# The tail of a two-layer attention kernel: normalising by tile, sharing the products, and experts from two rounded parts

## The chip, the cores and the metric

The kernel runs on one core of a Trainium2 chip. The metric is the device time of one execution in microseconds. Before the change three runs took 314.24 us (median), 313.40 and 314.36 us. Five engines work side by side, each with its own list of instructions that it takes in order: TensorE (PE, matmuls), VectorE (DVE), ScalarE (ACT), GpSimd (POOL) and SyncE (SP, which issues most DMAs). They wait for one another with semaphores. Nothing is ordered by a compiler; the order of every engine is written in the source.

## The reference, cut to what matters

Four batches of 256 tokens, 128 wide, pass two layers.

```python
x = x + cross_attention(layernorm(x), ctx)     # 16 heads of 64, 512 context rows, RoPE on the keys,
                                               # scores clipped to +-11, softmax, out @ Wo + bo
h = layernorm(x)                               # the second layer works on h, and its result is added to x
h1 = rmsnorm(h) * gamma1
q = h1 @ Wq + bq                               # 16 heads of 8
k, v = split((h1 @ Wdown + bdown) @ Wup + bup)
att = softmax(einsum('bthd,btgd->bthg', q, k) / sqrt(8))   # heads g against heads h, per token
r = h + (einsum('bthg,btgd->bthd', att, v) @ Wo2 + bo2)
h2 = rmsnorm(r) * gamma2
gate = softmax(h2 @ Wg + bg)                   # 8 experts
y = r + einsum('btd,edf,bte->btf', h2, We, gate)
out = x + y
```

## The kernel before, in words

The first layer runs in 32 slots, one for each pair of heads of each batch (8 slots a batch, some 8 us each). In a slot TensorE computes key, query and value projections for later slots, the scores of this pair in two halves, and the product of the previous pair's weights with the values (`times_values`). ScalarE takes exponentials, GpSimd clips them and adds the rotated keys, VectorE multiplies keys by cosine and sine and forms the low parts of operands. Where a product shall be nearly exact and faster than a plain fp32 matmul, the operand is kept as two rounded parts (dtype fp32r): `split3` then issues three matmuls, high by high, high by low, low by high.

The second layer of a batch is worked in small steps between the slots of the next batch. A table (`POST_STEPS`) puts TensorE's steps at places in the slots; `OWN_STEPS` does it for the other engines. The steps of batch 3, and the last of batches 1 and 2, have no slots left: they are the tail, from about 266 us on. `TAIL_STEPS` is TensorE's order there, and gives each step one of eight PSUM banks (0 is `side`, 1 and 2 are the two halves of `sc`, 3 `own_bank`, 4 and 5 `pj_k`, 6 `pv`, 7 `sums`). The other engines' tails are written out in `last_batches` (VectorE, GpSimd) and in ScalarE's block. A step `x/0` or `x/1` is that of one tile of 128 tokens. The steps in their order:

- `norm0` to `norm3`: reciprocals of the softmax sums (`recS`) are spread over the 128 partitions of a pair by a matmul with `spread`; VectorE multiplies `u` by them into `on`. Each step covers two pairs, all 256 tokens.
- `out_proj/t`: eight fp32 matmuls with `wo`, after which VectorE takes statistics, GpSimd the root, VectorE writes `hn`.
- `h_T`, `down`, `query`, `keyval2`: transposes and small products. VectorE (tile 1) and GpSimd (tile 0) multiply queries and keys into `prod`; `logits` sums tile 0's on TensorE by adding with the identity as an operand; `outputs` does it for the weighted values.
- `o_T`, `out_proj2`, `h2_T`, `gate`: output projection, root norm, transposed `h2T`, gate logits.
- `moe0` to `moe3`: tile 0's experts 0 to 3 and 4 to 7, then tile 1's. Each is one fp32 matmul of 128x512 with `fwe`. For batches 0 to 2 ScalarE multiplies each expert by its gate into `moe` and GpSimd adds them up (`add_experts`). For batch 3 VectorE adds them one by one straight from PSUM (`mix_tile`), in two sums, which `add_residuals` joins.

`made(name)` means that TensorE has finished a step, `taken(name)` that its bank has been read.

Of the kernel before, what the change touches and what calls it, by code (L numbers as in the profile page):

```python
# [28 lines left out]
fp32r = mybir.dt.float32r  # L29
ALU = mybir.AluOpType  # L30
# [20 lines left out]
G = 16  # L51
# [26 lines left out]
    ("norm0", LAST, 1), ("norm1", LAST, 2), ("norm2", LAST, 4), ("norm3", LAST, 5),  # L78
    ("out_proj/0", LAST, 6), ("out_proj/1", LAST, 7),
    ("h_T/0", LAST, 0), ("down/0", LAST, 1), ("query/0", LAST, 2), ("keyval2/0", LAST, 4),  # L80
    ("h_T/1", LAST, 5), ("down/1", LAST, 0), ("o_T", LAST - 1, 1), ("keyval2/1", LAST, 6), ("query/1", LAST, 7),
    ("out_proj2", LAST - 1, 2), ("logits", LAST, 4), ("h2_T", LAST - 1, 0), ("gate", LAST - 1, 5),
    ("moe0", LAST - 1, 1), ("moe1", LAST - 1, 6), ("moe2", LAST - 1, 0), ("outputs", LAST, 2),
    ("o_T/0", LAST, 4), ("out_proj2/0", LAST, 7), ("moe3", LAST - 1, 5), ("o_T/1", LAST, 1), ("out_proj2/1", LAST, 6),
    ("h2_T/0", LAST, 2), ("gate/0", LAST, 4), ("moe0", LAST, 0), ("h2_T/1", LAST, 1), ("moe1", LAST, 2),
    ("gate/1", LAST, 4), ("moe2", LAST, 7), ("moe3", LAST, 5),
# [24 lines left out]
    "root_norm": [(11, "end")],  # L111
    "gate_exps": [(13, None)],
# [11 lines left out]
}  # L124

# [112 lines left out]
def xattn_ffn(nc, x, ctx, cos, sin, ln_lat_g, ln_lat_b, ln_ctx_g, ln_ctx_b, Wq, Wkv, Wo, bo,  # L238
              gamma1, f_Wq, f_bq, f_Wdown, f_bdown, f_Wup, f_bup, f_Wo, f_bo, gamma2, f_Wg, f_bg, f_We, out):
    es = ExitStack()  # L240
    with es:
# [50 lines left out]
        fwe = sb("fwe", [128, NE, D])  # L292
# [48 lines left out]
        q2 = sb("q2", [128, D])  # L341
        dT = sb("dT", [L, NT])
# [5 lines left out]
        h2T = sb("h2T", [128, NT])  # L348
# [29 lines left out]
        ld = {n: sem(f"ld_{n}") for n in ("wk", "trig", "x", "wv", "wq", "bias", "wo", "ffn")}  # L378
# [57 lines left out]
        s_hn2 = sem("s_hn2")  # L436
        s_x23 = sem("s_x23")
# [8 lines left out]
        s_weigh_1a = sem("s_weigh_1a")  # L446
        s_gden = sem("s_gden")
# [28 lines left out]
        def taken(name, b):  # L476

            k, n = SIDE[name, b]
            return s_side_free[k], n + 1

# [23 lines left out]
        def _(sp):  # L504
# [44 lines left out]
            for j in range(NPAIR):  # L549
# [3 lines left out]
                for dst, src, name in later[3 * j - 3:3 * j] if j else ():  # L553
                    sp.dma_start(dst, src).then_inc(ld[name], 16)
# [11 lines left out]
        def _(pe):  # L566
# [69 lines left out]
            def times_values(j):  # L636
# [3 lines left out]
                if j:  # L640
                    pe.wait_ge(s_u, j)
# [1319 lines left out]
```

## Time and profile before

| what | value |
|---|---|
| median of three runs | 314.24 us |
| the profiled execution, whole | 312.95 us |
| its span (first to last instruction) | 311.2 us |
| granted TensorE clock over the span | 0.998 of 2.4 GHz |
| sums of batch 3's last pairs start (tail) | 266.27 us |

The profile is of one execution. A span of 311.2 us stands against a time of 312.95 us: 1.75 us lie outside. The busy shares are averages over the whole kernel. In the tail it is the order of each engine's list and the waits that count, so the timeline and the chain of waits are read there. A fp32 matmul is shown as two instructions.

### The profile page before, as it was taken

The page shows a single profiled execution, that of the slowest core. Times are in us where ns is not written, and L with a number is a line of the kernel's source. Part 1 is how long each engine was busy: PE and PEld are TensorE (multiplying, and loading weights), DVE is VectorE, ACT ScalarE, POOL GpSimd, SP SyncE. Part 2 cuts the span into 40 slices and gives each one's busy share as a digit, 9 for nine tenths or more (in the row PEclk, how much of TensorE's full clock was granted, in tenths as well). Part 3 has the DMA queues.
Part 4 walks back from the last instruction along what each step waited for, and adds up shares of the span by engine and source line. Part 5 has one row for each costly group of instructions (what it writes and reads, how often), then busy time and mean ns, then how long its engine had stood idle before and what let it go on. Part 6 is the DMA issues. An engine that isn't in the chain of part 4 may idle for free.

```text
span 311.2 us, 6616 instructions
## 1 busy us (share of the span) xinstructions
PE 292.3 (94%) x2482; PEld 204.0 (66%) x2482; DVE 243.4 (78%) x449; ACT 162.7 (52%) x326; POOL 209.0 (67%) x208
## 2 busy tenths in 40 slices
PE   7898999999999999999999999999999999899983
PEld 6776576666668666666687676556686665476651
DVE  3985998875875849899787798977847699687856
ACT  3446466667443734774426465774436368314741
POOL 6446775665573838686737578498827597968764
PEclk9999999999999999999999999999999999999999
DMA  7554412211210201111201111111101200000001
GB/s 218 179 151 114 123 38 57 62 36 44 60 28 9 52 17 36 35 36 36 51 19 34 37 34 36 33 38 34 36 0 37 53 1 2 0 19 0 1 2 34
DMA packets 16319, 14.24 MB, mean 46 GB/s; under 512 B 4832, under 2 KB 11808, under 8 KB 16288
## 3 DMA queue, kind: packets, MB, share of 16 engines
q1 hardware_dynamic: 14992, 13.49, 16.6%
q10 hardware_dynamic: 1296, 0.33, 0.5%
q8 instruction: 20, 0.33, 0.5%
q14 instruction: 11, 0.09, 0.1%
HBM read 4.89 MB, written 0.52 MB: 17 GB/s over the span
## 4 chain that ended last, share of the span: by engine, by line
PE 52%; DVE 21%; POOL 9%; issue 8%; ACT 5%; SPq 3%; DMA 2%; POOLq 0%; ACTq 0%; DVEq 0%
PE pv L645 10%; PE sc L631 9%; PE sums L666 6%; PE pj_k L569 4%; PE side L751 4%; DVE ks L1286 3%; PE pj_k L571 3%; PE pj_k L570 3%; SPq L536 3%; POOL moe L1868 3%; POOL e L1806 3%; PE side L827 2%; DVE ksin L1350 2%; DMA kswap<-ksin 2%; DVE kcos L1350 2%
## 5 line engine op out<-in xcount | busy, mean ns | idle before, releaser
L1806 POOL TENSOR_SCALAR e<-e 128x1024 f32<-128x1024 f32 x64 | 71.6, 1119 | 60.7 <-ACT e L944 47.6
L944 ACT ACTIVATE e<-sc 128x1024 f32<-128x1024 f32 x64 | 65.6, 1024 | 28.1 <-PE sc L631 28.0
L631 PEld LDWEIGHTS sc<-qs,ks 64*128 64x128 f32 x768 | 49.6, 185 | 21.7 <-issue 18.5
L645 PE MATMUL pv<-e,v 128*64 128x256 f32 x512 | 62.3, 385 | 1.6 <-POOL e L1806 0.8
L631 PE MATMUL sc<-qs,ks 64*128 64x256 f32 x768 | 62.5, 295 | 0.4 <-ACT e L944 0.2
L1799 POOL TENSOR_TENSOR krot<-kcos,kswap 128x512 f32<-128x512 f32 x32 | 45.2, 1411 | 9.8 <-DMA kswap<-ksin 7.0
L645 PEld LDWEIGHTS pv<-e,v 128*64 128x64 f32 x512 | 34.1, 136 | 24.2 <-issue 7.2
L952 ACT ACTIVATE u<-pv 128x256 f32<-128x256 f32 x32 | 12.3, 386 | 62.2 <-PE pv L645 55.5
L1286 DVE TENSOR_TENSOR ks<-krot,ks 128x512 fp32r<-128x512 f32 x32 | 33.6, 1051 | 0.1
L1350 DVE TENSOR_TENSOR ksin<-pj_k,sinT 128x512 f32<-128x512 f32 x32 | 21.9, 685 | 3.4 <-PE pj_k L571 3.2
L936 ACT ACTIVATE v<-pj_k 128x512 f32<-128x512 f32 x28 | 16.8, 598 | 14.3 <-PE pj_k L571 13.9
L666 PE MATMUL sums<-e,sum_rows 128*32 128x256 f32 x384 | 23.2, 382 | 0.6 <-POOL e L1806 0.6
L1350 DVE TENSOR_TENSOR kcos<-pj_k,cosT 128x512 f32<-128x512 f32 x32 | 21.8, 680 | 0.0
L921 ACT ACTIVATE ks<-krot 128x512 fp32r<-128x512 f32 x32 | 20.1, 629 | 1.2 <-POOL krot L1799 1.1
L1286 DVE TENSOR_TENSOR qs<-pj_k,qs 128x256 fp32r<-128x256 f32 x32 | 13.4, 418 | 9.1 <-ACT qs L927 9.1
L1360 DVE TENSOR_TENSOR moe<-e 128x512 f32<-128x512 f32 x16 | 12.5, 794 | 8.8 <-POOL e L1806 8.8
L666 PEld LDWEIGHTS sums<-e,sum_rows 128*32 128x32 f32 x384 | 11.2, 109 | 9.2 <-issue 1.1
L1595 DVE TENSOR_REDUCE own_bank<-prod 128x64 f32<-128x1024 f32 x14 | 16.6, 1216 | 0.1
L1868 POOL TENSOR_TENSOR moe<-moe 128x512 f32<-128x512 f32 (+2 forms) x18 | 15.4, 855 | 1.0
L569 PE MATMUL pj_k<-ctxT,wkA 128*128 128x512 f32 x32 | 14.3, 446 | 1.0 <-DVE kcos L1350 0.5
L1242 POOL TENSOR_TENSOR prod<-att,kv 128x1024 f32<-128x1024 f32 x6 | 14.6, 2435 | 0.6 <-ACT att L1053 0.3
L1234 POOL TENSOR_TENSOR prod<-q,kv 128x1024 f32<-128x1024 f32 x6 | 14.3, 2382 | 0.5
(289 smaller groups left out, 560.4 us busy)
## 6 DMA issues: line engine op xcount, KB each, us to landing
kswap<-ksin SPq DMA_DIRECT2D x126, 64.0 KB, 2.0
ctx_in<-in_ctx_dram SPq DMA_DIRECT2D x4, 256.0 KB, 3.4
prod<-in_L_xattn_Wkv_dram SPq DMA_DIRECT2D x2, 512.0 KB, 6.0
x_in<-in_x_dram SPq DMA_DIRECT2D x1, 512.0 KB, 6.0
prod<-in_L_xattn_Wq_dram SPq DMA_DIRECT2D x1, 512.0 KB, 6.8
wo<-in_L_xattn_Wo_dram SPq DMA_DIRECT2D x1, 512.0 KB, 4.4
fwe<-in_L_ffn_We_dram SPq DMA_DIRECT2D x1, 512.0 KB, 4.4
out_dram<-x_in SPq DMA_DIRECT2D x3, 128.0 KB, 1.8
```

Source lines behind the costliest of these rows:

```text
L569: nc.tensor.matmul(out_ap, w_hi, m_hi, start=True, stop=False)
L631: last = nc.tensor.matmul(sc[:, h, c * NT:(c + 1) * NT], ks[rows, j % 3, k_part, chunk], qs[rows, j % 2, q_part, :], start=(k_part + q_par ...
L645: last = nc.tensor.matmul(pv_bank[DH * h:DH * h + DH, 0:NT], v[:, c, col:col + DH], e[:, j % 3, h, c, :], start=(c == 0), stop=(c == SC - 1))
L666: last = nc.tensor.matmul(sum_bank[32 * g:32 * g + 32, 0:NT], w, e_added[:, pair % 2, c, g % 2, :] if j < PAIRS else e[:, pair % 3, g % 2, ...
L921: nc.scalar.activation(ks[:, j % 3, 0, :], krot[:, j % 2, :], ACT.Copy).then_inc(s_khi, 1)
L936: nc.scalar.activation(v[:, c, 512 * half:512 * half + 512], value_bank(n)[:, :], ACT.Copy).then_inc(s_v, 1)
L944: nc.scalar.activation(e[:, j % 3, :, 2 * half:2 * half + 2, :].rearrange("p h c n -> p h (c n)"), sc[:, :, :], ACT.Exp, scale=SCALE).then ...
L1286: return nc.vector.tensor_tensor(dst, whole, f(hi), ALU.subtract)
L1350: nc.vector.tensor_tensor(dst[:, j % 2, :], key_bank(j)[:, :], trig[:, :], ALU.mult).then_inc(s_kmul, 1)
L1799: nc.gpsimd.tensor_tensor(krot[:, j % 2, :], kcos[:, j % 2, :], kswap[:, j % 2, :], ALU.add)\
L1806: nc.gpsimd.tensor_scalar(a, a, EXP_HIGH, EXP_LOW, ALU.min, ALU.max).then_inc(s_clip, 1)
L1868: own(nc.gpsimd.tensor_tensor(moe[:, t, 0:n, :], moe[:, t, 0:n, :], moe[:, t, n:2 * n, :], ALU.add))
```

## The change

1. `norm0` to `norm3` of batch 3 cover four pairs and one tile each (four matmuls of 128 columns in place of two of 256). `out_proj/0` waits for `norm0` and `norm1` alone.
2. The last pair's `times_values` writes into bank 1 and no longer waits for ScalarE's copy of the pair before it.
3. VectorE reduces batch 2's outputs (two `reduce_half`) ahead of the reciprocals. The statistics of both tiles stand ahead of both `norm_tile`.
4. Query times key: VectorE takes half of tile 0 and half of tile 1, GpSimd the other halves. ScalarE copies tile 1's queries to `q2_last` for GpSimd.
5. Experts in all batches: `h2T` and the expert weights are kept in two rounded parts (`h2S`, `fweS`). ScalarE writes `h2T` and then the high part; VectorE writes the low part (`split_h2`); `moe` is a `split3`. The weights land in `prod`'s first part and are split in slots 4 (ScalarE) and 8 (GpSimd). `h2T` now lies in the memory of `fbup_r`.
6. Tile 1 of batch 2 is mixed by VectorE (`mix_before`) and no longer by ScalarE and GpSimd.
7. Batch 3: `gate/1` stands ahead of `moe1`. ScalarE weighs tile 0's experts 4 to 7 and tile 1's expert 7 (`weigh`), VectorE adds the others. GpSimd adds tile 1's residual beforehand and sums tile 0's.
8. ScalarE's order in the tail: `weight_exps(LAST, 0)` ahead of `h2_T`; `o_T/1` and `second_square(1)` ahead of `root_norm_tile(0)`.

The diff, cut to its core:

```diff
-    ("h2_T/0", LAST, 2), ("gate/0", LAST, 4), ("moe0", LAST, 0), ("h2_T/1", LAST, 1), ("moe1", LAST, 2),
-    ("gate/1", LAST, 4), ("moe2", LAST, 7), ("moe3", LAST, 5),
+    ("h2_T/0", LAST, 7), ("gate/0", LAST, 4), ("moe0", LAST, 0), ("h2_T/1", LAST, 1), ("gate/1", LAST, 7),
+    ("moe1", LAST, 2), ("moe2", LAST, 6), ("moe3", LAST, 5),
...
+    "split_h2": [(13, "early")],
...
+                if j == NPAIR - 1:
+                    pe.wait_ge(s_exp, 2 * NPAIR)
+                elif j:
                     pe.wait_ge(s_u, j)
...
-                        last = nc.tensor.matmul(dst, spread[:, p, :], recS[:, 1, :], start=True, stop=True)
+                    for p in range(2 * i, 2 * i + 2) if b < LAST else range(4 * (i % 2), 4 * (i % 2) + 4):
+                        dst = side[:, NT * (p % 2):NT * (p % 2) + NT] if b < LAST else side[:, D * (p % 4):D * (p % 4) + D]
+                        of = recS[:, 1, :] if b < LAST else recS[:, 1, D * (i // 2):D * (i // 2) + D]
+                        last = nc.tensor.matmul(dst, spread[:, p, :], of, start=True, stop=True)
...
-                    w = fwe[:, 4 * half:4 * half + 4, :].rearrange("d e f -> d (e f)")
-                    last = nc.tensor.matmul(side[:, :], h2T[:, 128 * t:128 * t + 128], w, start=True, stop=True)
+                    pe.wait_ge(s_h2lo, b + 1 + (t if b == LAST else 0))
+                    cols, w = slice(128 * t, 128 * t + 128), slice(512 * half, 512 * half + 512)
+                    last = split3(side[:, :], h2S[:, 0, cols], h2S[:, 1, cols], fweS[:, 0, w], fweS[:, 1, w])
...
-                    nc.scalar.activation(h2T[:, to], side[:, at], ACT.Copy, scale=GAM2).then_inc(free, 1)
+                    nc.scalar.activation(h2T[:, to], side[:, at], ACT.Copy, scale=GAM2)
+                    nc.scalar.activation(h2S[:, 0, to], side[:, at], ACT.Copy, scale=GAM2).then_inc(free, 1)
...
+            def weigh(t, experts, done):
+                act.wait_ge(s_y, TT * (LAST - 1) + 1)
+                act.wait_ge(t_gate, t + 1)
+                act.wait_ge(*made(f"moe{2 * t + 1}", LAST))
+                side = side_banks[SIDE[f"moe{2 * t + 1}", LAST][0]]
+                for i in experts:
+                    nc.scalar.activation(moe[:, t, i, :], side[:, D * (i - 4):D * (i - 4) + D], ACT.Copy,
+                                         scale=gate_last[:, t, i:i + 1]).then_inc(done, 1)
...
+            weight_exps(LAST, 0)
             take("h2_T", before)
-            weight_exps(LAST, 0)
+            weight_exps(LAST, 1)
             gate_exps_last()
-            weight_exps(LAST, 1)
...
             take("o_T/0", LAST)
             second_square(0)
+            take("o_T/1", LAST)
             second_residual(0)
-            take("o_T/1", LAST)
+            second_square(1)
             root_norm_tile(0)
-            second_square(1)
             take("h2_T/0", LAST)
...
+            def mix_second():
+                dve.wait_ge(t_residual, 1)
+                dve.wait_ge(t_gate, 2)
+                dve.wait_ge(*made("moe2", LAST))
+                for n, i in enumerate(MIX_ORDER):
+                    if i == 1:
+                        dve.wait_ge(t_weigh_last, 1)
...
             def last_batches():
-                reciprocals(LAST)
                 reduce_half(0, 0)
                 own(reduce_half(0, 1))
+                reciprocals(LAST)
...
                 residual_statistics(0)
-                dve.wait_ge(s_prod2, LAST)
-                reduce_half(1, 0)
-                norm_tile(0)
                 residual_statistics(1)
+                norm_tile(0)
+                norm_tile(1)
                 own(reduce_half(1, 1))
...
+                first_products(nc.vector, 0, side_banks[k][:, 0:D]).then_inc(t_prod_dve, 1)
                 keys_and_values(1)
...
                 reduce_half(1, 0)
-                divide_first()
                 own(reduce_half(1, 1))
+                divide_first()
...
+            def split_h2(name, b):
+                dve.wait_ge(*taken(name, b))
+                split_lo(h2S[:, 1, cols], h2T[:, cols], h2S[:, 0, cols]).then_inc(s_h2lo, 1)
...
-                for part in range(2):
-                    first_products(nc.gpsimd, part).then_inc(t_prod, 1)
+                first_products(nc.gpsimd, 1, q2[:, :]).then_inc(t_prod, 1)
+                pool.wait_ge(t_q, 2)
...
+                products(nc.gpsimd, LAST, 1, 1, q2_last).then_inc(t_prod_1, 1)
                 pool.wait_ge(s_ss2, LAST + 1)
                 mean_square_root(rr2, ss2).then_inc(s_rr2, 1)
```

How the instructions now stand at three places. First TensorE at the head of the tail, from the last sums to the output projection, before:

```order
L666 MATMUL sums<-e,sum_rows 32x256 x16
L645 MATMUL pv<-e,v 64x256 x16
L738 MATMUL sc<-recS,spread 128x256 x4
L738 MATMUL pj_k0<-recS,spread 128x256 x2
L738 MATMUL pj_k1<-recS,spread 128x256 x2
L747 MATMUL pv<-x_in,ident 128x128
L751 MATMUL pv<-wo,on 128x128 x8
L747 MATMUL sums<-x_in,ident 128x128
L751 MATMUL sums<-wo,on 128x128 x8
```

and now:

```order
L696 MATMUL sums<-e,sum_rows 32x256 x16
L675 MATMUL pv<-e,v 64x256 x8
L675 MATMUL sc<-e,v 64x256 x8
L772 MATMUL pv<-recS,spread 128x128 x4
L772 MATMUL sc<-recS,spread 128x128 x4
L772 MATMUL pj_k0<-recS,spread 128x128 x4
L772 MATMUL pj_k1<-recS,spread 128x128 x4
L781 MATMUL sc<-x_in,ident 128x128
L787 MATMUL sc<-wo,on 128x128 x8
L781 MATMUL sums<-x_in,ident 128x128
L787 MATMUL sums<-wo,on 128x128 x8
```

The last `times_values` went to `sc`, and each norm step has four 128-column matmuls in place of two of 256; all sixteen still stand ahead of the first `out_proj`.

Second VectorE at the same place, from the last pair's second-layer sums (`aden`) to the statistics of the first layer's result, before:

```order
L1584 TENSOR_REDUCE aden<-att 128x16
L1585 RECIPROCAL aden<-aden 128x16
L1369 RECIPROCAL sums<-sums 128x256
L1371 CAST recS<-sums 128x256
L1373 SCALAR_TENSOR_TENSOR recS<-recS,odd,sums 128x256
L1595 TENSOR_REDUCE own_bank<-prod 128x64 x2
L1598 TENSOR_TENSOR o2<-own_bank,aden 128x128
L1408 TENSOR_TENSOR on<-u,sc 128x512 x2
L1408 TENSOR_TENSOR on<-u,pj_k0 128x512
L1408 TENSOR_TENSOR on<-u,pj_k1 128x512
L1483 BN_STATS f_stat<-pv 128x6
```

and now:

```order
L1702 TENSOR_REDUCE aden<-att 128x16
L1703 RECIPROCAL aden<-aden 128x16
L1713 TENSOR_REDUCE own_bank<-prod 128x64 x2
L1422 RECIPROCAL sums<-sums 128x256
L1424 CAST recS<-sums 128x256
L1426 SCALAR_TENSOR_TENSOR recS<-recS,odd,sums 128x256
L1716 TENSOR_TENSOR o2<-own_bank,aden 128x128
L1713 TENSOR_REDUCE own_bank<-prod 128x64
L1464 TENSOR_TENSOR on<-u,pv 128x4x128
L1464 TENSOR_TENSOR on<-u,sc 128x4x128
L1464 TENSOR_TENSOR on<-u,pj_k0 128x4x128
L1464 TENSOR_TENSOR on<-u,pj_k1 128x4x128
L1544 BN_STATS f_stat<-sc 128x6
```

The reductions of `prod` moved ahead of the reciprocals, and a third one ahead of the multiplications into `on`.

Third ScalarE late in the tail, around the output projection of batch 3's two tiles (`hn2,ss2` is a square with its sum, `hn2<-..,rr2` the root norm, `h2T` and `h2S` the transposed copies; `h2T` prints as `fbup_r` now), before:

```order
L1005 ACTIVATE oT<-pj_k0 128x128
L1100 ACTIVATE hn2,ss2<-sums 128x128
L1104 ACTIVATE xl<-sums 128x128
L1005 ACTIVATE oT<-sc 128x128
L1122 ACTIVATE hn2<-sums,rr2 128x128
L1100 ACTIVATE hn2,ss2<-pv 128x128
L1010 ACTIVATE h2T<-sc,vec 128x128
L1104 ACTIVATE xl<-pv 128x128
L1122 ACTIVATE hn2<-pv,rr2 128x128
```

and now:

```order
L1048 ACTIVATE oT<-pj_k0 128x128
L1145 ACTIVATE hn2,ss2<-sc 128x128
L1048 ACTIVATE oT<-sc 128x128
L1149 ACTIVATE xl<-sc 128x128
L1145 ACTIVATE hn2,ss2<-pv 128x128
L1168 ACTIVATE hn2<-sc,rr2 128x128
L1053 ACTIVATE fbup_r<-sums,vec 128x128
L1054 ACTIVATE h2S<-sums,vec 128x128
L1168 ACTIVATE hn2<-pv,rr2 128x128
L1149 ACTIVATE xl<-pv 128x128
```

Tile 0's root norm, `hn2<-sc,rr2`, now stands behind tile 1's square `hn2,ss2<-pv`, and the transposed copy is written twice.

## Rows read from the trace of the kernel before

**Rows 1.** The page: busy time by engine, and the chain that ended last.
```profile
PE 292.3 (94%) x2482; PEld 204.0 (66%) x2482; DVE 243.4 (78%) x449; ACT 162.7 (52%) x326; POOL 209.0 (67%) x208
PE 52%; DVE 21%; POOL 9%; issue 8%; ACT 5%; SPq 3%; DMA 2%; POOLq 0%; ACTq 0%; DVEq 0%
```

**Rows 2.** The chain in order of time: start us, length us, what.
```profile
261.04 1.12 PE side L827 x2
...
277.18 1.79 PE sums L751 x16
291.27 0.86 PE pv L827 x2
...
292.99 3.58 PE sc L789 x32
```

**Rows 3.** Timeline, TensorE: start us, length us, engine, line, operation, tiles.
```profile
193.61 0.39 PE L570 MATMUL pj_k<-wvS,ctxT 128*128 128x512 f32 x1
193.84 0.40 PE L571 MATMUL pj_k<-wvS,ctxT 128*128 128x512 f32 x1
...
212.94 0.28 PE L569 MATMUL pj_k<-latT,wqS 128*128 128x256 f32 x1
213.06 0.28 PE L570 MATMUL pj_k<-latT,wqS 128*128 128x256 f32 x1
```

**Rows 4.** Timeline, batch 1 near 249 us: ScalarE and TensorE [idle before].
```profile
249.27 0.47 ACT L1010 ACTIVATE h2T<-side,vec 128x256 f32<-128x256 f32 x1
249.88 0.58 PE L821 MATMUL side<-fwg,h2T 128*128 128x8 f32 x4 [0.18 <-ACT h2T L1010]
```

**Rows 5.** Timeline near 191 us, and this subtraction's lengths in ns (min/median/max).
```profile
191.26 1.13 POOL L1806 TENSOR_SCALAR e<-e 128x1024 f32<-128x1024 f32 x1
191.52 1.14 DVE L1286 TENSOR_TENSOR latT<-latT_f,latT 128x256 fp32r<-128x256 f32 x1
...
L1286 DVE TENSOR_TENSOR latT<-latT_f,latT x4: 426/784/1162, 17.6 to 191.5; 128x256 fp32r<-128x256 f32 x4
```

**Rows 6.** Timeline, the head of the tail: TensorE and VectorE.
```profile
268.34 1.77 DVE L1369 RECIPROCAL sums<-sums 128x256 f32<-128x256 f32 x1 [2.07 <-PE sums L666]
270.66 1.95 PE L645 MATMUL pv<-e,v 128*64 128x256 f32 x16 [0.57 <-ACT u L952]
271.00 2.35 DVE L1595 TENSOR_REDUCE own_bank<-prod 128x64 f32<-128x1024 f32 x2
...
278.53 0.40 DVE L1490 TENSOR_SCALAR hn<-pv,f_mv,rr 128x128 f32<-128x128 f32 x1
280.67 0.41 DVE L1490 TENSOR_SCALAR hn<-sums,f_mv,rr 128x128 f32<-128x128 f32 x1
```

**Rows 7.** Timeline: GpSimd, VectorE and ScalarE in the middle of the tail.
```profile
282.02 4.01 POOL L1253 TENSOR_TENSOR prod<-q,kv 128x1024 f32<-128x1024 f32 x2 [0.46 <-DVE kv L1517]
284.25 2.36 DVE L1234 TENSOR_TENSOR prod<-sums,kv 128x1024 f32<-128x1024 f32 x2
286.38 0.70 POOL L1772 TENSOR_TENSOR rr<-rr,half_p 128x2 f32<-128x2 f32 x1
289.92 4.23 POOL L1262 TENSOR_TENSOR prod<-att,kv 128x1024 f32<-128x1024 f32 x2 [1.50 <-ACT att L1053]
296.60 0.29 DVE L1475 TENSOR_TENSOR o<-sc,aden 128x128 f32<-128x128 f32 x1 [0.27 <-PE sc L789]
299.75 0.36 ACT L1122 ACTIVATE hn<-sums,rr 128x128 f32<-128x128 f32 x1
300.43 0.28 ACT L1100 ACTIVATE hn<-pv 128x128 f32<-128x128 f32 x1 [0.32 <-PE pv L807]
```

**Rows 8.** Timeline: the last instruction of VectorE and the last store.
```profile
308.06 0.45 DVE L1272 TENSOR_TENSOR x_in<-x_in,xl 128x128 f32<-128x128 f32 x1
308.92 0.37 SPq L561 DMA_DIRECT2D out_dram<-x_in  x1
```

**Rows 9.** The page: GpSimd's multiplication of queries and keys.
```profile
L1234 POOL TENSOR_TENSOR prod<-q,kv 128x1024 f32<-128x1024 f32 x6 | 14.3, 2382 | 0.5
```

More of the change, by code:

```diff
@@ L748, in side_product @@
                         for p in range(PAIRS):
-                            if t == 0 and p % 2 == 0:
+                            if tile and p % 4 == 0:
+                                pe.wait_ge(*taken(f"norm{2 * t + p // 4}", b))
+                            elif not tile and t == 0 and p % 2 == 0:
                                 pe.wait_ge(*taken(f"norm{p // 2}", b))
@@ L786, in side_product @@
                     for i in range(n):
-                        if i % (n // 2) == 0:
-                            pe.wait_ge(t_prod if name == "logits" else t_prod2, 2 * i // n + 1)
+                        if name == "outputs" and i % (n // 2) == 0:
+                            pe.wait_ge(t_prod2, 2 * i // n + 1)
+                        elif name == "logits" and i == 0:
+                            pe.wait_ge(t_prod_dve, 1)
+                        elif name == "logits" and i == n // 2:
+                            pe.wait_ge(t_prod, 1)
                         last = nc.tensor.matmul(side[:, 0:width], ident[:, :], prod[:, 0, width * i:width * i + width],
@@ new lines, in mix_before @@
+            def mix_before():
+                b = LAST - 1
+                dve.wait_ge(s_gate, TT * (b + 1))
+                dve.wait_ge(*taken("out_proj2", b))
+                dve.wait_ge(s_hn2, b + 1)
+                for i in range(NE):
+                    name = f"moe{2 + i // 4}"
+                    row = xl[:, b % 2, 1, :] if i % 2 else x_in[:, TT * b + 1, :]
+                    if i % 4 == 0:
+                        dve.wait_ge(*made(name, b))
+                    if i == 5:
+                        dve.wait_ge(*taken("moe2", b))
+                    elif i >= 2:
+                        dve.wait_ge(s_mix_before, i - 1 if i < 5 else i - 2)
+                    k = SIDE[name, b][0]
+                    nc.vector.scalar_tensor_tensor(row, side_banks[k][:, D * (i % 4):D * (i % 4) + D],
+                                                   gate[:, 1, i:i + 1], row, ALU.mult, ALU.add)\
+                        .then_inc(s_side_free[k] if i % 4 == 3 else s_mix_before, 1)
@@ L1664, in second_layer @@
                         root_norm(b)
+                    if stands("split_h2", b, slot, when):
+                        split_h2("h2_T", b)
                     if stands("gates", b, slot, when):
```

213 lines of the change are left out of this document (141 added, 72 removed).

## The prediction

> **What bounds the kernel now.** I read the busy shares first, then the chain of waits, then the timeline of the tail. TensorE is busy for 94% of the span and holds 52% of the chain that ended last, VectorE 21% and GpSimd 9% of it [rows 1]: up to about 266 us matmuls follow each other nearly without a gap, behind that short steps hand over from engine to engine. The chain shows both kinds: an expert step of batch 1, the output projection, the long addition of the weighted values with the identity, 3.58 us [rows 2]. Each part is worth what it does to the step that is waited for, so the sum needs two pieces: what reaches 266 us (the body), and the walk from there to the last store (the tail).
>
> **Body.** An fp32 expert step holds TensorE for 0.86 us [rows 2]. One rounded matmul of 512 columns starts 0.23 us behind another [rows 3], so three take 0.70: 0.16 us less for each step. Batch 0's four steps and three of batch 1's, one of them in the chain [rows 2], stand where TensorE is waited for: 7 x 0.16 = -1.1 us. Against it, ScalarE writes the transposed tile twice and frees the bank at the second copy. One takes 0.47 us, and in batch 1 the gate's matmul waited for it already [rows 4]; a second adds 0.38 there, by the pace of such copies. In batch 0 there is room for about half. So +0.55 for both. The splitting of the weights (ScalarE about 1.1 us once, GpSimd about 2.4 us once, for 1024 columns) lies in slots where both engines idle longer than that between exponentials: I take 0, up to +0.5.
>
> VectorE's new subtraction for the low part reads two tiles from SBUF. The like of it took 1.14 us and ended 0.27 us behind a GpSimd instruction that had begun 0.26 us before it, where the shortest took 0.43 [rows 5]. In batch 1 it meets GpSimd's addition of the rotated keys. VectorE has little slack at the end of the body, since the change also puts 2.35 us of reductions ahead of the reciprocals, into an idle time of 2.07 [rows 6]. So +0.2, between 0 and +0.9. Body: -1.1 + 0.55 + 0.2 = -0.35 us.
>
> The Trainium skill (SBUF — State Buffer, "Who interferes with whom") says that a VectorE instruction with two SBUF inputs contends with a GpSimd instruction that reads SBUF, and that the order of issue decides who blocks. The trace agrees [rows 5]: by that rule each such meeting costs VectorE the rest of GpSimd's instruction.
>
> **Tail, the head.** The last value product starts at 270.66 after 0.57 us of waiting for ScalarE's copy [rows 6]; without that it ends near 271.9, not 272.5. VectorE's two reductions come first, so the reciprocals start at 268.65 and not 268.34, and the rows to spread are ready at 271.4, not 271.1. The sixteen spreading matmuls can start at 272.0. No row shows a rounded matmul of 128 columns. Bounds from both sides: half the pace of the 256-column one, 0.12 us [rows 3], so 0.06 and 1.0 us in all; or the rate of plain fp32, 8 matmuls of 128 columns in 1.79 us [rows 2], so 0.22 and 3.5 us. Fp32 instructions with 8 columns still follow each other at 0.11, (0.58 - 0.26) / 3 [rows 4], which looks like the price of loading 128x128 weights. I take 0.11, so 1.8 us. `out_proj/0` then runs from 273.85 to 275.9 (bias 0.22, matmuls 1.79) and `out_proj/1` to 277.9, 1.05 us earlier than before. Tile 1's statistics are out at 278.4, tile 0's `hn` is written behind them at 278.45 (278.53 before), tile 1's at 279.4 (280.67) [rows 6]. Tile 0 gains 0.1 us, tile 1 1.3.
>
> **Tail, the middle.** From there TensorE's small steps close up, and batch 2's `out_proj2` ends about 0.7 us earlier. GpSimd's two products took 4.01 us, VectorE's two 2.36 [rows 7]. In halves, VectorE is done with its first by 282.8 and GpSimd by 283.6 instead of 286.03, so `logits` runs without waiting and ends about 0.8 us earlier. But GpSimd's half of tile 1, 2.38 us [rows 9], stands ahead of batch 2's root, which ends no earlier than its 287.08 [rows 7]. The exponential of tile 0 lets GpSimd's weighted values start 0.8 us before 289.92 [rows 7].
>
> Then the gain is given back three times. (a) ScalarE takes `h2_T` behind that exponential, and twice: the gate's matmuls start at 289.9, 0.65 us later than before, and VectorE's subtraction meets GpSimd's weighted values, 2.1 us each [rows 7]: it may wait to 291.2, so VectorE's own chain is 0.4 us late. (b) VectorE divides tile 0's outputs behind both reductions: 291.8 for the first weighted product, two of 1.18, 0.2 for the gate's reciprocal, sums 0.75, reductions 2.35: 297.5, against 296.60 [rows 7]. (c) Tile 0's root norm stood at 299.75; it now waits for tile 1's square, at 300.43 before [rows 7] and near 300.9 now, and comes at 301.3: +1.5 us. The second copy adds 0.3.
>
> **Tail, the end.** Tile 0's transposed copies are ready at 302.7, gate and `moe0` go to 303.9, tile 1's transpose and copies to 304.9, its gate takes 0.45, then three rounded steps of 0.7: the last experts are there at 307.6. ScalarE weighs one (0.3), VectorE adds five more of 0.26 and the last sum of 0.45: 310.0 with the gaps, where it ended at 308.51 [rows 8]. GpSimd's sums for tile 0, 0.74 + 0.46 + 0.46 behind ScalarE's four weighings, end at 309.5, and SyncE issues the last store at 309.9; before, at 308.92 [rows 8], it ended the span 2.3 us later. ScalarE's own store, half as large, is issued 1.5 us later than it was and lands at about the same time. GpSimd's sum of batch 2, which ended the kernel, is gone; this is late next. So +1.0 by the store, and +1.2 with the half of the meeting in (a) that the small steps behind it do not take up.
>
> **Sum.** -0.35 + 1.2 = +0.85 us on an execution of 312.95 us, a span of 311.2. The runs' median is 1.3 us above that execution; the same difference on it gives 315.1. I say 315.2.
>
> **The rivals.**
> 1. *Narrow rounded matmuls at the fp32 rate.* 0.22 us each; all sixteen stand ahead of `out_proj/0`, which ends at 277.5, and the rest follows 1.6 us later. For it: plain fp32 takes 0.22 at this width [rows 2]. Against: at 256 columns nothing of the sort shows [rows 3]. Time 316.8 us.
> 2. *The gain at the front lives: faster.* The place is ScalarE's list at tile 0's root norm. If tile 1's square is done before the root of tile 0 is out, the new place costs nothing. It decides at 0.85 us: tile 1's square has to follow tile 0's by less than that, where 2.2 us lay between them. If it does, and VectorE and GpSimd do not meet, 0.9 of the middle's gain stays: -0.35 - 0.9. Time 313.0 us.
> 3. *Nothing to be seen.* TensorE's list has gaps in the tail that take up (a) to (c), and the last store comes when it did; only the body counts. Time 314.1 us.
>
> **How the numbers follow.** What a measurement of this kernel can tell from no change is 0.3%, 0.94 us. The forecast has 0.38, rival 1 0.29, rival 2 0.18, rival 3 0.15. The forecast lies at that bound, and by the bounds of its terms it is good to 0.8 us each way: 0.20 of it counts as slower, 0.18 as the same. Slower 0.20 + 0.29 = 0.49; same 0.18 + 0.15 = 0.33; faster 0.18. The range reaches from just under rival 2 to just over rival 1 and leaves out the far halves of both: 312.9 to 317.2 us. The forecast's own range is 314.3 to 316.0.
>
> **What would show it.** The sixteen spreading matmuls tell rival 1 at once: 1.8 us or 3.5. Right if tile 0's root norm on ScalarE starts directly behind tile 1's square; if the low part in the tail takes over 0.6 us; if an expert step holds TensorE for 0.7 us; and if the last store is issued about 43.6 us behind the start of the body's last sums (42.6 before). Wrong if VectorE divides tile 0's outputs earlier against those sums than before, or if they start more than 1 us earlier or at all later than 266.3 us.

## The result and the profile after

The changed kernel takes 319.02 us (median of 4 runs, 318.13 to 319.64), the kernel before 314.06 (4 runs, 313.40 to 314.36). The ratio is 1.0164, 95% interval 1.0141 to 1.0187: slower by 5.0 us. The prediction had the direction as its likeliest class, but its 315.2 us and its range, 312.9 to 317.2, miss the time.

The profiled execution took 319.13 us, with a span of 317.3. Its page answers [rows 1]:

```profile
span 317.3 us, 6695 instructions
PE 293.8 (93%) x2506; PEld 211.1 (67%) x2506; DVE 248.2 (78%) x457; ACT 164.3 (52%) x330; POOL 211.8 (67%) x210
PEclk9799999999999999999999999999999999999797
PE 49%; DVE 25%; POOL 7%; issue 7%; ACT 5%; DMA 4%; SPq 3%; ACTq 0%; POOLq 0%; DVEq 0%
```

TensorE is as busy as before. VectorE has a larger part of the chain, 25%. The third line is the granted clock in 40 slices, and it has 7s near the start and twice near the end. The windows over those places give the clock itself (columns: stretch, its length, busy time and count of TensorE, its weight loads, VectorE, ScalarE, GpSimd; then granted clock, DMA share, GB/s). The changed kernel:

```profile
9.00:12.00 3.00, 3.00 (x16) 3.00 (x15) 2.86 (x10) 0.78 (x1) 0.00 (x0) 0.50 0.72 207
290.00:295.00 5.00, 2.41 (x15) 1.78 (x14) 4.15 (x7) 2.49 (x10) 4.21 (x4) 1.00 0.00 0
295.00:300.00 5.00, 5.00 (x29) 4.77 (x28) 4.62 (x7) 2.66 (x10) 4.47 (x6) 0.66 0.01 3
300.00:309.00 9.00, 6.53 (x39) 4.80 (x37) 4.68 (x18) 3.75 (x16) 3.60 (x9) 1.00 0.00 0
309.00:313.00 4.00, 4.00 (x13) 2.88 (x12) 2.40 (x10) 1.50 (x6) 1.29 (x3) 0.57 0.00 0
```

From 290 to 295 us TensorE works 2.41 of 5.00 us, and in the next stretch its clock is at 0.66 on average: 1.2 GHz for most of it. From 300 to 309 it works 6.53 of 9.00, and then it is at 0.57. The kernel before ran its tail up to 306 us at a granted clock of 1.00. The same two stretches of it:

```profile
290.00:295.00 5.00, 5.00 (x29) 3.56 (x29) 4.49 (x9) 4.00 (x18) 4.93 (x3) 1.00 0.00 0
295.00:300.00 5.00, 4.28 (x25) 2.90 (x24) 3.69 (x7) 1.80 (x9) 4.24 (x7) 1.00 0.01 3
```

TensorE's timeline of the changed kernel shows what the waits were and what ran slow behind them (start us, length us, what, idle before; the gate's four small matmuls show as eight instructions):

```profile
292.49 0.39 PE L860 MATMUL sc<-fbg_less,ident 128*128 128x8 f32 x2 [1.47 <-ACT h2S L1054]
294.33 0.47 PE L597 MATMUL sc<-fweS,h2S 128*128 128x512 f32 x1 [0.78 <-DVE h2S L1339]
295.86 5.30 PE L829 MATMUL sums<-prod,ident 128*128 128x128 f32 x32
305.32 0.30 PE L704 MATMUL sums<-ident,hn 128*128 128x128 f32 x1 [0.81 <-ACT hn L1168]
306.34 0.39 PE L860 MATMUL pj_k<-fbg_less,ident 128*128 128x8 f32 x2 [0.71 <-ACT h2S L1054]
308.73 0.39 PE L860 MATMUL sums<-fbg_less,ident 128*128 128x8 f32 x2 [0.71 <-ACT h2S L1054]
309.20 0.64 PE L597 MATMUL sc<-fweS,h2S 128*128 128x512 f32 x1
309.63 0.63 PE L598 MATMUL sc<-fweS,h2S 128*128 128x512 f32 x1
```

The long addition takes 5.30 us. In the kernel before it took 3.73 in the same view (3.58 in the chain, [rows 2]). Rounded 512-column matmuls follow each other at 0.43 us at the end, and at 0.23 in [rows 3]. Every one of these waits ends with work that the change added or moved: the second copy `h2S`, the low part, the root norm in its new place.

### The profile page after: what moved, and what is told of

Same layout as the page of the kernel before. It is cut to its first block, busy times and chain, and to the rows that moved or that the text cites. A ratio compares the mean times of both kernels' runs of the same rounds, so it can differ in the third digit from the quotient of the medians.

```text
span 317.3 us, 6695 instructions
## 1 busy us (share of the span) xinstructions
PE 293.8 (93%) x2506; PEld 211.1 (67%) x2506; DVE 248.2 (78%) x457; ACT 164.3 (52%) x330; POOL 211.8 (67%) x210
## 4 chain that ended last, share of the span: by engine, by line
PE 49%; DVE 25%; POOL 7%; issue 7%; ACT 5%; DMA 4%; SPq 3%; ACTq 0%; POOLq 0%; DVEq 0%
PE pv L675 8%; PE sc L659 7%; PE sums L696 5%; PE side L787 4%; PE pj_k L597 4%; DVE ks L1339 3%; SPq L562 3%; PE pj_k L598 2%; PE pj_k L599 2%; DVE ksin L1403 2%; POOL e L1926 2%; POOL moe L2006 2%; DMA kswap<-ksin 2%; DMA sin_in<-in_L_xattn_sin_dram 2%; ACT moe L1068 2%
## 5 line engine op out<-in xcount | busy, mean ns | idle before, releaser
L675 PE MATMUL pv<-e,v 128*64 128x256 f32 x496 | 60.4, 385 | 1.6 <-POOL e L1926 1.5
L675 PEld LDWEIGHTS pv<-e,v 128*64 128x64 f32 x496 | 32.8, 136 | 23.6 <-issue 6.2
L1339 DVE TENSOR_TENSOR ks<-krot,ks 128x512 fp32r<-128x512 f32 x32 | 32.6, 1019 | 0.1
L2006 POOL TENSOR_TENSOR moe<-moe 128x512 f32<-128x512 f32 (+2 forms) x15 | 13.1, 871 | 1.3 <-ACT moe L1068 0.4
```

Source lines behind the costliest of these rows:

```text
L675: last = nc.tensor.matmul(outputs_bank(j)[DH * h:DH * h + DH, 0:NT], v[:, c, col:col + DH], e[:, j % 3, h, c, :], start=(c == 0), stop=(c ...
L1339: return nc.vector.tensor_tensor(dst, whole, f(hi), ALU.subtract)
L2006: own(nc.gpsimd.tensor_tensor(moe[:, t, 0:n, :], moe[:, t, 0:n, :], moe[:, t, n:2 * n, :], ALU.add))
```

## The experiments

The theories: A, TensorE's clock falls behind the new waits and most of the loss is that; B, the new waits and orders alone; C and F, the inputs land later at the start; D, the split of the experts costs in the body and in the middle; E, the places (a) to (c) of the prediction, each by its size; G, the part of the low part's 1.72 us that lies in the chain. All runs in one table. "Tail" is the span less the start of the body's last sums, "low" the stretches of the profiled execution at 1.2 GHz, without what lies behind TensorE's last work.

```
                                median  runs  first scores  last sums  tail  low
before                          314.06     4     20.23       266.27   44.9  none
after                           319.02     4     21.57       268.69   48.6  9-12, 296-299, 309-312
e1  after, fillers              315.94     9     21.24       268.60   46.1  8-11
e2  after, fillers at start     317.97     4     20.86       267.16   49.2  293-296, 306-end
e3  after, fp32 experts         318.34     4     21.08       267.45   47.9  304-310
e4  before, split experts       319.03     4     20.25       267.15   49.2  294-297
e5  e3 with fillers             313.92    10     21.38       267.50   45.1  8-11
e6  e5, three orders put back   313.29    10     21.00       267.25   44.3  none
e7  before, room and semaphores 314.25     8     21.37       267.63   44.9  8-12
e8  before, fillers             313.70    10     22.37       268.72   45.1  10-13
e9  e1 without one low part     315.38    10     21.36       268.58   45.7  none
e10 e1, three orders put back   315.09     6     21.19       268.09   45.4  none
e11 e1, body with fp32 matmuls  315.40     7     21.01       267.92   46.1  none
e12 after, fillers in middle    317.80     4     21.88       268.87   48.1  9-12, 306-312
```

The kernel before, run beside them, had medians of 313.87 to 313.93 us.

**e1, unused matmuls ahead of the waits.** A filler is one 128x128 matmul of the identity into the bank that the next step will write anyway.

```diff
+TAIL_FILL = {("h_T/0", LAST): 4, ("gate", LAST - 1): 6, ("moe0", LAST - 1): 3,
+             ("h2_T/0", LAST): 3, ("gate/0", LAST): 3, ("gate/1", LAST): 3}
...
             for name, b, k in TAIL_STEPS[1:]:
...
+                if (name, b) in TAIL_FILL:
+                    bank_ready(name, b, *SIDE[name, b])
+                    keep_busy(TAIL_FILL[name, b], side_banks[k])
                 side_product(name, b)
```

> The changed kernel with unused 128x128 matmuls on TensorE ahead of six of its waits in the tail (4 ahead of tile 0's h_T, 6 ahead of batch 2's gate, 3 ahead of its moe0, 3 each ahead of the last batch's h2_T/0, gate/0 and gate/1). Theory A (the clock: after these waits TensorE runs at 1.2 GHz for 3.4 us in the middle and 3.3 us at the end): the stretches from 295 to 300 and from 309 to 313 us run at 2.4 GHz, the additions of the outputs take 3.6 us and not 5.3, an expert step at the end 0.7 and not 1.3; 1.7 + 1.7 us less: 315.6 to 316.2 us. Theory B (the new waits and the order of ScalarE's and VectorE's lists alone; other engines would be waited for at either clock): 318.5 to 319.5 us.

Measured 315.94 us, ratio to before 1.0068 (1.0049 to 1.0088): 3.1 us of the 5.0 are gone (by the two ratios and their intervals 3.0 us, give or take 0.9), as theory A has it. The same windows and the same matmuls of this kernel:

```profile
290.00:295.00 5.00, 4.51 (x32) 3.90 (x32) 4.24 (x7) 2.40 (x10) 4.22 (x4) 1.00 0.00 0
295.00:300.00 5.00, 5.00 (x39) 4.51 (x37) 4.86 (x9) 2.67 (x10) 4.47 (x6) 1.00 0.01 3
300.00:309.00 9.00, 8.57 (x51) 6.96 (x51) 5.90 (x23) 4.44 (x20) 3.88 (x10) 1.00 0.00 0
```

```profile
292.40 0.39 PE L861 MATMUL sc<-fbg_less,ident 128*128 128x8 f32 x2
294.24 0.47 PE L598 MATMUL sc<-fweS,h2S 128*128 128x512 f32 x1
295.72 3.73 PE L830 MATMUL sums<-prod,ident 128*128 128x128 f32 x32
307.62 0.48 PE L598 MATMUL sc<-fweS,h2S 128*128 128x512 f32 x1
307.94 0.39 PE L599 MATMUL sc<-fweS,h2S 128*128 128x512 f32 x1
```

Against the last sums, the gate and the first expert step start when they did: the waits are all still there (theory B's point), only filled. What changed is the clock behind them. Against the last sums, VectorE divides tile 0's outputs 1.5 us earlier (31.06 us behind them, 32.57 without fillers), and the last store of ScalarE comes 3.0 us earlier (43.6, 46.7). So the clock cost 1.5 us in the middle and 1.5 at the end. (The two tails in the table differ by 2.5 us only, since in e1 the last store is followed by 2.5 us until the span ends, in the changed kernel by 2.0.)

**e2, more unused matmuls at the start.**

```diff
-WARM_UP = {"cos_T": 11, ...
+WARM_UP = {"cos_T": 15, ...
```

> The changed kernel with 15 and not 11 unused matmuls ahead of the first transpositions, to bridge the 1.55 us of TensorE's waiting from 6.2 to 7.7 us. Theory A (the clock fell for that wait): no stretch at 1.2 GHz between 9 and 12 us, the first scores start 0.5 us earlier: 318.5 us. Theory C (the inputs land 1.0 us later in the changed kernel and that is all): the wait is filled, the granted clock may stay, but the first scores stay within 0.2 us of 21.57: 318.8 to 319.0 us.

Measured 317.97 us, below both expectations. The stretch at 1.2 GHz at the start is gone, as A said. The first scores came at 20.86, and the body took up another 0.4 us by its fourth pair, but e7 and e8 show that such shifts also come and go by themselves. With 4 runs, how much of the 1.0 us is due to the fillers stays open. The tail was as slow as ever, with two stretches at 1.2 GHz.

**e3, the change without the split.**

```diff
-last = split3(side[:, :], h2S[:, 0, cols], h2S[:, 1, cols], fweS[:, 0, w], fweS[:, 1, w])
+last = nc.tensor.matmul(side[:, :], h2T[:, cols], fwe[:, w], start=True, stop=True)
```

The second copy, the low parts and the weights' split are left out with it.

> The changed kernel without the rounded parts: the experts' weights in one fp32 tile, fp32 matmuls, no second copy of h2_T, no subtractions for low parts. Theory D (the split costs in the body: weights' low part 0.37 us, second copy 0.2, low parts and their meetings with GpSimd the rest; in the tail 1.9 us of waiting between gate and moe0, and with it the stretch at 1.2 GHz in the middle): 1.1 less in the body, 2 less in the middle: 315.5 to 316.5 us. By the prediction's own account the split gave 0.35 us in the body and took about 0.6 in the tail: 318.5 to 319.2 us.

Measured 318.34 us (316.67, 317.18, 319.50, 319.72). By its time this speaks against D, but the clock mixes in: the first two runs had a mean granted clock of 0.987, the other two 0.976. In the profiled one the middle is at 2.4 GHz, and from 304 to 310 us, behind the new waits of the end, fp32 expert steps run at half clock. The body is where D put it: from the fourth pair's queries to the last sums it takes 0.25 us more than before. The price of the split had to be measured with the clock held: e5.

**e4, the kernel before with the split alone.** Its tail's order is unchanged.

```diff
                 less_maximum(LAST, 1)
+                split_h2("h2_T", before)
                 gate_logits_of(before)
```

> The kernel before with the rounded parts for the experts alone (weights' split, second copy, low parts; the tail's order as before, with the low part of batch 2 behind tile 1's less_maximum, those of the last batch ahead of gate_logits(0) and mix_tile(0)). Theory D: 1.1 us more by the end of the body and 1 to 2 more in the tail: 316 to 317 us. By the prediction: 313.7 to 314.5 us. If the inputs land 1.0 us later here too (first scores at 21.5, not 20.2), the place of the new tiles or the new load is what delays them.

Measured 319.03 us, ratio 1.018 (1.0139 to 1.0222): the split alone costs as much as the whole change. 0.9 us are lost in the body, 4.2 in the tail. There the gate's matmuls start at 290.50 us, but VectorE is still at tile 1's second reduction and its `less_maximum` and comes to the low part at 292.24. TensorE waits 1.81 us for it; the clock falls behind that, and the additions of the outputs, 3.73 before, take 4.46. My expectation had taken the wait from the changed kernel, where the order is another.

**e5, fp32 experts and fillers.**

```diff
+TAIL_FILL = {("h_T/0", LAST): 4, ("gate", LAST - 1): 4, ("h2_T/0", LAST): 3,
+             ("gate/0", LAST): 2, ("gate/1", LAST): 2}
```

> The changed kernel with fp32 experts (no rounded parts at all) and with unused matmuls ahead of five of TensorE's waits in the tail (4, 4, 3, 2, 2). Theory A and D together (the clock costs up to 3.4 us, the split costs 1.1 us in the body and the late gate and low part in the middle): no stretch at 1.2 GHz in the tail, 314.2 to 314.8 us. If the clock were only a sign of the waits and not their price: 317 to 318 us, as with fp32 experts alone.

Measured 313.92 us, ratio 1.0006 (0.9988 to 1.0024). This is 0.3 us under what was expected. So with the clock held the split costs 315.94 - 313.92 = 2.0 us (1.9 by the ratios, give or take 0.8), and all the rest of the change, what the head and the middle gain and what (a) to (c) cost, comes to nothing that can be seen. 2.0 and 3.1 make up the 5.0 us. This is one way to share them out. Taken in the other order, the split away first (e3) and the fillers second (e5), they are 0.7 and 4.4 us, since the clock falls without the split as well, and further in two of e3's four runs. The two causes do not simply add up.

**e6, e5 with the places (a) to (c) put back.**

```diff
-            weight_exps(LAST, 0)
             take("h2_T", before)
+            weight_exps(LAST, 0)
...
             second_residual(0)
-            second_square(1)
             root_norm_tile(0)
+            second_square(1)
...
                 reduce_half(1, 0)
-                own(reduce_half(1, 1))
                 divide_first()
+                own(reduce_half(1, 1))
```

> The same with three places of the tail put back: ScalarE takes h2_T ahead of tile 0's exponential, VectorE divides tile 0's outputs between the two reductions, ScalarE's root norm of tile 0 stands ahead of tile 1's square. Theory E (the prediction's places (a) to (c), each by its size in the traces: gate 0.45 us earlier, the division 0.5, the root norm 0.5, in one chain): 0.8 to 1.2 us less than the kernel that it is made from: 313.2 to 313.8 us. Rival: each place is followed by another wait (outputs' additions, tile 1's own chain), and the three together give under 0.3 us.

Measured 313.29 us, ratio 0.9981 (0.9962 to 1.0000): 0.6 us less than e5, a little under the expectation. It is the fastest kernel of the study, at the edge of what can be told from the kernel before. VectorE and ScalarE there:

```profile
296.83 0.29 DVE L1531 TENSOR_TENSOR o<-sums,aden 128x128 f32<-128x128 f32 x1 [1.09 <-PE sums L826]
```

```profile
300.14 0.37 ACT L1166 ACTIVATE hn<-sc,rr 128x128 f32<-128x128 f32 x1
300.67 0.28 ACT L1143 ACTIVATE hn<-pv 128x128 f32<-128x128 f32 x1 [0.15 <-PE pv L844]
```

The division comes 29.6 us behind the last sums (30.2 in e5, 30.3 before) and now waits 1.09 us for TensorE. That may be where the expected rest of the gain stopped; no run takes this wait away. The root norm is out of the way when tile 1's square can start.

**e7, the kernel before with an unused tile and eight unused semaphores.**

```diff
+        q2_last = sb("q2_last", [128, D])
...
+        unused = [sem(f"s_unused{i}") for i in range(8)]
```

> The kernel before with one more 512-byte tile (q2_last, never used) and eight more semaphores (never used). Theory F (the inputs land 0.9 us later in the changed kernel for what it adds to the layout, since four kernels with its tail all read the sine table at 6.8 to 7.1 us and two without it at 5.9 and 6.1): first scores at 21.0 to 21.6 us and 0.8 to 1.2 us more: 314.8. Rival (chance, or the tail's instructions): first scores at 20.2, 314.0 us.

**e8, the kernel before with fillers.**

```diff
+TAIL_FILL = {("gate", LAST - 1): 3, ("gate/0", LAST): 2, ("gate/1", LAST): 1, ("h_T/0", LAST): 1}
```

> The kernel before with unused matmuls ahead of four of TensorE's waits in the tail (1 ahead of tile 0's h_T, 3 ahead of batch 2's gate, 2 and 1 ahead of the last batch's gates). Theory A (the unused matmuls help only where the clock fell, and in this kernel it did not ahead of 310 us): 313.6 to 314.3 us, no change. If they help by something else than the clock: under 313.2 us.

e7 had its first scores at 21.37, as F said, but 314.25 us and a ratio of 1.0003 (0.9985 to 1.0021), which F excludes. e8, with neither tile nor semaphores, started later than any of them, and its profiled run was its slowest of ten (315.61). Its first scores and its sine table:

```profile
22.37 0.98 PE L632 MATMUL sc<-qs,ks 64*128 64x256 f32 x12
```

```profile
sin_in<-in_L_xattn_sin_dram ACTq DMA_DIRECT2D x1, 64.0 KB, 6.4
```

The table took 6.4 us to land, 4.7 in the profiled execution of before and 5.7 in that of the changed kernel. So the start differs from run to run by up to 2.1 us in kernels whose start is the same code, and the kernel before was profiled at an early one, which is of the size of its 1.3 us below the median. Theory F falls. As for the fillers, 313.70 us and 1.0005 (0.9985 to 1.0025) say that fillers, fewer here than in e1, give nothing that can be seen where the clock had not fallen.

**e9, e1 without the low part of batch 2 in the tail** (its experts multiply with a stale low part).

```diff
                 less_maximum(LAST, 1)
-                split_h2("h2_T", before)
                 gate_logits_of(before)
```

> The changed kernel with the six groups of unused matmuls, and without VectorE's low part of batch 2 in the tail (its experts multiply with the stale low part of batch 1; all matmuls stay). Theory G (the meeting of place (a), 1.72 us of VectorE beside GpSimd's weighted values, lies in the chain, but VectorE then waits for the gate's matmuls): VectorE divides tile 0's outputs 0.6 us earlier against the sums, 315.3 us, with 315.9 for the fillers alone. If all 1.72 us were in the chain: 314.3; if none: 315.9.

Measured 315.38 us, ratio 1.0050 (1.0030 to 1.0070): 0.56 less than e1, but the two intervals overlap, so the time alone doesn't tell theory G from none. It speaks against all 1.72 us, which would give 314.3. The traces decide. In the place of the 1.7 us VectorE waits 1.53 us for the gate's matmuls:

```profile
293.48 0.17 DVE L1572 TENSOR_REDUCE gmax<-sc 128x2 f32<-128x16 f32 x1 [1.53 <-PE sc L862]
```

`gmax` started at 294.02 in e1. Against the last sums it comes 0.5 us earlier, and the division of tile 0's outputs and the last store 0.35 us. That is theory G's mechanism at a smaller size than its 0.6.

**e10, e1 with the places (a) to (c) put back**, the edit of e6 on the rounded experts.

> The changed kernel with the six groups of unused matmuls and the three places put back (h2_T ahead of tile 0's exponential on ScalarE, the division between the reductions, tile 0's root norm ahead of tile 1's square), rounded experts kept. With fp32 experts the three gave 0.6 us. Theory E: 0.5 to 1.0 us here too, 315.0 to 315.4 us. Rival (with the split the low part decides the middle, whatever stands ahead of it): 315.8 us or more.

Measured 315.09 us, ratio 1.0030 (1.0006 to 1.0054): 0.85 less than e1, and 0.7 in the profiled tails. Theory E holds. The rival, that the low part decides whatever stands ahead of it, falls in an instructive way. The low part in the changed kernel, and the GpSimd instructions that it met:

```profile
292.46 1.72 DVE L1339 TENSOR_TENSOR h2S<-fbup_r,h2S 128x256 fp32r<-128x256 f32 x1 [0.41 <-ACT h2S L1054]
```

```profile
291.78 4.40 POOL L1322 TENSOR_TENSOR prod<-att,kv 128x1024 f32<-128x1024 f32 x2 [0.70 <-ACT att L1097]
```

and in e10, where ScalarE makes `h2_T` first and GpSimd gets its input later:

```profile
291.37 0.42 DVE L1343 TENSOR_TENSOR h2S<-fbup_r,h2S 128x256 fp32r<-128x256 f32 x1
```

1.72 us or 0.42, for the same subtraction: here it starts 0.3 us ahead of GpSimd's product (291.68).

**e11, e1 with single fp32 matmuls for the experts of batches 0 and 1** (with the rounded high part of the weights, so their low part is left out there).

```diff
+                    if b < LAST - 1:
+                        last = nc.tensor.matmul(side[:, :], h2T[:, cols], f(fweS[:, 0, w]), start=True, stop=True)
+                    else:
+                        last = split3(...
```

> The changed kernel with the six groups of unused matmuls; batches 0 and 1 take one fp32 matmul for each expert step (with the rounded weights' high part alone, so the weights' low part is left out there), no second copy of h2_T and no low part of it in the body. The weights are still split. Theory D: of about 0.9 us that the body lost by the split, 0.37 (GpSimd's subtraction for the weights) stays and 0.5 goes: last sums 0.5 us nearer to the fourth pair's queries, 315.4 us. By the prediction's account of these two terms (seven faster steps 1.1 us less, copies and low parts 0.75 more), 0.35 us more: 316.3.

Measured 315.40 us, ratio 1.0043 (1.0023 to 1.0062). The 316.3 of the prediction's terms lies outside. It is 0.54 less than e1, as D has it, though the two intervals overlap. The last sums start at 267.92, 231.9 us behind the fourth pair's queries; in e1 it is 232.2, and 232.3 on average in the seven kernels with the whole split. So the traces show 0.3 to 0.4 us.

**e12, fillers in the middle alone.**

```diff
+TAIL_FILL = {("gate", LAST - 1): 6, ("moe0", LAST - 1): 3}
```

> The changed kernel with unused matmuls ahead of batch 2's gate (6) and its moe0 (3) alone. If each stretch at 1.2 GHz has its own waits: outputs' additions at 2.4 GHz, the experts of the end still at 1.2: 317.3 us. If the fall at the end only follows from the one in the middle: 315.9, as with all six groups.

Measured 317.80 us, ratio 1.0115 (1.0087 to 1.0143): 1.2 less than the changed kernel, where 1.7 were expected. The windows:

```profile
295.00:300.00 5.00, 5.00 (x39) 4.71 (x39) 4.86 (x8) 2.75 (x11) 4.48 (x6) 1.00 0.01 3
309.00:313.00 4.00, 3.72 (x9) 2.33 (x8) 1.74 (x6) 1.57 (x7) 1.74 (x4) 0.50 0.00 0
```

The middle is at 2.4 GHz, the end at 1.2: each stretch has its own waits.

## Why the prediction was wrong, step by step

**The step that failed.** The walk through the tail took every duration of a matmul from rows at 2.4 GHz and never asked whether the clock would stay there. It found the waits: the gate 0.65 us later, the low part delayed by GpSimd, the root norm late. It priced each as a delay of what stands behind it. It left out that TensorE, idle for 1.47 and 0.78 us with only the gate's four small matmuls (eight instructions) in between, would then run at 1.2 GHz. The same happened behind the waits of 0.81, 0.71 and 0.71 us near the end. That is 3.1 us, shown by e1, with a control in e8. No rival had it either. The Trainium skill (TensorE: Matmul & The Clock Gate, "Part 1: The HAM clock gate") says that the throttled state is the default and that activity releases it; the trace agrees, 1.2 GHz behind both groups of waits. By that page the prediction should have carried a rival of this kind.

**The walk itself, at full clock,** can be read from e1. Predicted: the last store issued 43.6 us behind the last sums. In e1:

```profile
312.17 0.43 SPq L590 DMA_DIRECT2D out_dram<-x_in  x1
```

312.17 - 268.60 = 43.6. The tail's +1.2 us is 46.1 - 44.9 = 1.2. The sum came out better than its terms: some of them below are off by 0.2 to 0.4 us, and they happen to cancel.

**Head of the tail: right.** The sixteen spreading matmuls of the changed kernel, in four steps:

```profile
274.17 0.65 PE L772 MATMUL pv<-recS,spread 128*128 128x128 f32 x4
274.66 0.61 PE L772 MATMUL sc<-recS,spread 128*128 128x128 f32 x4
275.11 1.05 PE L772 MATMUL pj_k<-recS,spread 128*128 128x128 f32 x8
276.00 0.44 PE L781 MATMUL sc<-x_in,ident 128*128 128x128 f32 x2
```

1.83 us for sixteen, 0.11 each, and 1.8 predicted. Rival 1 falls. Against the last sums, tile 0's `hn` comes 0.25 us earlier (0.1 predicted) and tile 1's 1.35 (1.3); compare [rows 6] with

```profile
280.70 0.40 DVE L1551 TENSOR_SCALAR hn<-sc,f_mv,rr 128x128 f32<-128x128 f32 x1
281.74 0.41 DVE L1551 TENSOR_SCALAR hn<-sums,f_mv,rr 128x128 f32<-128x128 f32 x1 [0.64 <-POOL rr L1884]
```

**Middle: right in kind, a little too large.** Tile 0's logits are less their maximum 0.56 us earlier (0.8 predicted). (a) The gate's matmuls start 0.8 us later (0.65), and the low part takes 1.72 us; e9's trace prices it at 0.35 in the chain (0.4). (b) The division is 0.7 us later in e1 (0.9). (c) The root norm of tile 0 comes 1.15 us later against the sums in e1 (1.5), directly behind tile 1's square. In the changed kernel's own trace:

```profile
304.55 0.28 ACT L1145 ACTIVATE hn<-pv 128x128 f32<-128x128 f32 x1 [0.41 <-PE pv L847]
304.73 0.19 ACT L1145 ACTIVATION_READ_ACCUMULATOR hn<-pv 128x1 f32 x1
304.82 0.36 ACT L1168 ACTIVATE hn<-sc,rr 128x128 f32<-128x128 f32 x1
```

**Body: the wrong sign.** Predicted -0.35 us, measured +0.9 (e4, whose start agrees with that of before to 0.02 us: 267.15 - 266.27). The last sums start at 268.69 in the changed kernel, later than 266.3, and the prediction had named that as a sign of being wrong. Part of it is the late start of that execution (first scores at 21.57 and 20.23). Part of the 0.9 isn't the split's either: between the sixteenth and the seventeenth pair e4 falls back by 0.2 us, and so do e3 and e7, which have no split, but not e5, e6 and e8. From the fourth pair's queries to the last sums the seven kernels with the whole split take 0.7 to 1.0 us more than before, 0.8 on average, the five without it -0.05 to 0.3, 0.1 on average. So the split costs some 0.7 us in the body. Two of the prediction's terms were mis-sized, one was right, and the low parts (+0.2) weren't measured by themselves.

The weights' split was taken at 0, with 0.5 as its bound. GpSimd's subtraction stood where nothing waited for GpSimd, but VectorE's instruction beside it took 1.30 us, and VectorE was waited for. The changed kernel, GpSimd, VectorE (0.88 us for this subtraction before) and TensorE:

```profile
84.36 2.37 POOL L2067 TENSOR_TENSOR fweS<-prod,fweS 128x1024 fp32r<-128x1024 f32 x1
```

```profile
85.97 1.30 DVE L1339 TENSOR_TENSOR ks<-krot,ks 128x512 fp32r<-128x512 f32 x1
```

```profile
87.93 0.50 PE L772 MATMUL side<-recS,spread 128*128 128x256 f32 x2 [0.31 <-DVE on L1469]
```

From the queries of the eleventh pair to those of the twelfth, the changed kernel falls back by another 0.37 us against before, and each of the eight profiled kernels with the split weights does so by 0.35 to 0.38; in the five without it the two stay within 0.01. The prediction had the rule of such meetings in it [rows 5] and used it for the low parts alone.

The second copy was put at 0.38 us in batch 1 and half of that in batch 0. In batch 0 the gate waits for it and 0.22 us are lost:

```profile
183.80 0.58 PE L861 MATMUL side<-fwg,fbup_r 128*128 128x8 f32 x4 [0.22 <-ACT h2S L1054]
```

In e4 batch 1's gate waits 0.55 us, 0.18 before [rows 4]: 0.37. This term was right.

The gain of seven faster expert steps, 1.1 us, is the largest error. Batch 0's four gave their 0.64: e4 is 0.76 us behind before ahead of them and 0.09 behind at pair 26's queries. But the next value product then waited for GpSimd's clipping, which had not become faster, and e4 was 0.41 behind again. Batch 1's three gave 0.15 us, since a faster step only arrives sooner at ScalarE, which still weighs the experts of the step before. TensorE in e4:

```profile
214.92 1.95 PE L654 MATMUL pv<-e,v 128*64 128x256 f32 x16 [0.46 <-POOL e L1833]
260.01 0.50 PE L578 MATMUL side<-fweS,h2S 128*128 128x512 f32 x1 [0.23 <-ACT moe L1037]
262.20 0.50 PE L578 MATMUL side<-fweS,h2S 128*128 128x512 f32 x1 [0.21 <-ACT moe L1037]
266.25 0.51 PE L578 MATMUL side<-fweS,h2S 128*128 128x512 f32 x1 [0.28 <-ACT moe L1037]
```

The first three of these waits were not there before. e11 takes copies, low parts and faster steps out of the body together and is 0.54 us faster, so their balance was a loss, of 0.3 to 0.4 us by the traces.

**The rivals.** The second, that the front's gain lives, needs the root norm free, and (c) shows that it was not. The third is refuted by the time, though e5 shows it for the change without split and clock. Its 314.1 was also 0.2 us off its own terms: the body alone gives 314.24 - 0.35 = 313.9. The sum of the true terms: 0.7 to 0.9 in the body, 1.2 in the tail at full clock, 3.1 for the clock, 5.0 to 5.2 us against 5.0 measured.

## What to carry to other kernels

When a change adds waits to TensorE in a stretch of small matmuls, read the granted clock there first and give the case that it halves a price: everything on TensorE that follows, twice. Unused matmuls into the bank that comes next fill such waits at no cost that could be seen here (e8), and they also tell a wait's own cost from the clock's. A step that is made faster is worth only the distance to the next engine's wait, and an instruction on GpSimd that nobody waits for can still hold up VectorE.

## What the runs showed that was not expected

The first scores of one and the same code came anywhere in 2 us (20.23 in the profiled execution of before, 21.37 and 22.37 in e7 and e8), with the sine table landing 4.7 to 6.4 us after its issue. At the start the clock was at 1.2 GHz for about 3 us in some executions (e8, from 10 to 13) and not in others. How much it costs there was not measured by itself.

The length of one wait was no guide. In e12 waits of 0.81 and 0.71 us were followed by the fall at 306.3, and six microseconds at 1.2 GHz. In the changed kernel the same two waits were not, and the clock fell only at 309.4, behind a third of 0.71. In e3 a wait of 1.09 us ahead of the gate led to no fall, and in e4 one of 0.81 near the end did not; in the kernel before none was longer than 0.56 in these places, and none did. e3's four runs fell into two groups, 316.9 and 319.6 us, at clocks of 0.987 and 0.976: near the edge the same program goes either way.
